# Second edge stage of a four-layer graph network: VectorE scales the gathered rows of group g + 2 ahead of the last sums of group g

## The reference, cut to what matters

```python
norm_src = clip(out_deg, 1) ** -0.5
h = nfeat * norm_src[:, None]
agg = segment_sum(h[src], dst)             # over 25000 edges
conv = agg @ W * norm_dst[:, None] + b     # norm_dst = clip(in_deg, 1) ** -0.5
sfeat = (nfeat @ W + b) / (in_deg + 1)
esum = segment_sum(efeat @ We + be, dst)
out = conv + sfeat + esum / clip(in_deg, 1)
```

## Time and profile before

| | us |
|---|---|
| median of 3 runs | 12018.62 |
| lowest, highest | 12002.51, 12023.15 |
| profiled execution | 11995.85 |
| its span on the core | 11994.1 |
| mean granted TensorE clock | 0.687 |

### The profile page before, as it was taken

How to read it: one execution, slowest core, us unless ns; L and a number is a source line. 1 busy time by engine, 2 the same in 40 slices (tenths; PEclk the granted TensorE clock), 3 DMA queues, 4 the chain that set the end, 5 groups by cost and what they waited for, 6 DMA issues and landing times. The chain is left out here.

```text
span 11994.1 us, 149789 instructions
## 1 busy us (share of the span) xinstructions
PE 6782.4 (57%) x33931; PEld 5074.2 (42%) x33931; DVE 6277.9 (52%) x20811; ACT 1432.6 (12%) x3027; POOL 6513.3 (54%) x6508
## 2 busy tenths in 40 slices
PE   3544547665567656567656667655567266570072
PEld 2333214443356444356443446544346144560051
DVE  5576545555545555545555554555554755550067
ACT  0022003000002000001100000200000500351005
POOL 4667351555643556553455654356554555676646
PEclk8755767766677766667776667776667577785555
DMA  3143001344422344421334431334431511692106
GB/s 121 38 159 122 2 2 54 70 82 83 84 47 65 69 79 84 82 56 40 87 76 83 84 63 30 92 73 84 83 72 31 181 48 52 146 200 37 24 20 267
DMA packets 526027, 950.80 MB, mean 79 GB/s; under 512 B 187011, under 2 KB 269788, under 8 KB 525604
## 3 DMA queue, kind: packets, MB, share of 16 engines
q0 software_dynamic: 192000, 330.22, 18.4%
q1 hardware_dynamic: 316196, 516.19, 13.8%
q10 hardware_dynamic: 17664, 102.61, 2.1%
HBM read 502.28 MB, written 458.64 MB: 80 GB/s over the span
## 5 line engine op out<-in xcount | busy, mean ns | idle before, releaser
L965 POOL DMA_INDIRECT G<-tab,gidx x4000 | 3805.8, 951 | 3554.8 <-issue 1897.5
L1401 PE MATMUL PS<-G,M 128*128 128x128 f32 x8000 | 2131.7, 408 | 1945.6 <-DVE G L396 1626.8
L1401 PEld LDWEIGHTS PS<-G,M 128*128 128x128 f32 x8000 | 1722.9, 276 | 2402.2 <-DVE G L396 1827.1
L1386 PE MATMUL PS<-G,lring 128*1 128x128 f32 x8000 | 1498.3, 348 | 224.9 <-DMA G<-tab,gidx 184.4
L398 DVE SCALAR_TENSOR_TENSOR G<-G,whole,PS 1x128 f32<-1x128 f32 (+1 forms) x3300 | 1103.5, 334 | 823.7 <-issue 128.2
L1346 DVE TENSOR_TENSOR Y<-PS,big 128x512 f32<-128x512 f32 x800 | 553.4, 692 | 1334.0 <-remote 1079.2
L419 DVE TENSOR_SCALAR M<-keyrow,keycol,wccol 128x128 f32 (+1 forms) x4004 | 1135.3, 364 | 29.3 <-issue 8.2
L1386 PEld LDWEIGHTS PS<-G,lring 128*1 128x1 f32 x8000 | 719.6, 100 | 779.7 <-DMA G<-tab,gidx 226.7
L1355 ACT COPY big<-PS 128x512 f32 x200 | 117.0, 585 | 5453.5 <-remote 3647.8
L1397 PE MATMUL PS<-M,G 128*128 128x128 f32 x1600 | 486.3, 401 | 437.9 <-DVE G L396 431.6
L1066 POOL DMA_INDIRECT Y<-pair_d,G x400 | 402.3, 1006 | 359.7 <-DMA pair_d<-UT 207.4
(11 more groups left out here) (498 smaller groups left out, 11639.0 us busy)
## 6 DMA issues: line engine op xcount, KB each, us to landing
tab<-Y SPq DMA_DIRECT2D x1000, 256.0 KB
big<-agg SPq DMA_DIRECT2D x90, 832.0 KB, 12.7
G<-tab,gidx POOLq DMA_INDIRECT x4000
big<-x SPq DMA_DIRECT2D x60, 832.0 KB, 8.8
xt_d<-big SPq DMA_DIRECT2D x30, 858.0 KB, 13.6
x2n<-big ACTq DMA_DIRECT2D x30, 838.5 KB
big<-x2n SPq DMA_DIRECT2D x30, 838.5 KB
agg<-big ACTq DMA_DIRECT2D x30, 832.0 KB
```

Source lines behind the costliest of these rows:

```text
L965: pool.indirect_dma_start(G[:, t % RG, 0:D], None, tab_in(k), bass.IndirectOffsetOnAxis(ap=gidx[:, t:t + 1], axis=0)).then_inc(l_got[t % R ...
L1386: nc.tensor.matmul(PS[0:1, CAR, j, :], lring[:, GR * h + j:GR * h + j + 1], G[:, s, 0:D], start=True, stop=True).then_inc(l_row, 1)
L1401: ins = nc.tensor.matmul(PS[:, SUM + h, j, :], M[:, GR * h + j, :], G[:, s, 0:D], start=True, stop=True)
```

## The change

VectorE's order in this stage is written out. `normed(0, 0)`, `summed(0, 0)` and `normed(0, 1)` stand ahead of the loop. In the loop, for each g: `summed` of g + 1, a wait for c_sum of g, `normed` of g + 2, `finished` of g. Behind the loop: `summed` of group 49, `finished` of 48 and of 49. The other engines' programs stay as they are.

```diff
-                def to_sums(i, h):
-                    normed(i, h)
-                    summed(i, h)
-                two_stages(dve, to_sums, finished)
+                normed(0, 0)
+                summed(0, 0)
+                normed(0, 1)
+                with dve.Fori(0, IT - 1) as i:
+                    for h in range(2):
+                        summed(i + h, 1 - h)
+                        steady(dve, 2 * i + h + 1)
+                        dve.wait_ge(c_sum, 2 * i + h + 1)
+                        normed(i + 1, h)
+                        finished(i, h)
+                summed(IT - 1, 1)
+                finished(IT - 1, 0)
+                finished(IT - 1, 1)
```

## The result

The kernel after took 12139.5 us (median of 4 runs, 12124.9 to 12145.4), the kernel before 12020.9 beside it: a ratio of 1.0098, with a 95% interval of 1.008 to 1.0115, so some 96 to 138 us slower. The forecast was 12151 us.

A forecast was written before the change was run, and what follows sets the result against it. No engine is full, so a loop of waits sets the pace; the change closes it in one group, 16.69 us against 13.88, 47 times: +132 us on the median scale's 12018.6, 12151 us, range 12100 to 12222.

The forecast's parts named there:

- The loop: Second edge stage: Y, scatter, gather, landing, scaling, last sums, Y close in one group, 16.69 us against 13.88; chance 0.77.
- first scatter to last gather: POOL's issues in the loop, from the first scatter to the start of the last gather: 9.05 us.
- gather to scaling: Start of the last gather on POOL to VectorE's scaling of its tile: 2.53 us.
- scaling and index copy: VectorE's scaling of the last tile plus the small copy L1694: 0.38 us.
- bound of 4.05 us for the landing: Upper end of gather start to scaling, from the stage's start; would add 71 us, giving 12222.
- The sum: Whole change: 2.81 us a group, 47 times, +132 us, with the ends' +1.0 and -1 cancelling.
- Both ends: Ahead of Y of group 0, +1.0 us for one more scaling; Y of 47 to Y of 49, -1 (0 to -2.5).
- The added wait: VectorE's wait for c_sum of g before scaling g + 2: costed at 0, if c_sum comes within 8.6 us of Y.
- late signals of TensorE: Rival: TensorE's late signals set the new pace, 20.2 us a group, +298 us, 12317 us; chance 0.11.
- room that a loop of 16.7 us leaves: VectorE's running sums have 4 us before the first gathered tile, 8 before the last; L1718 about 13 us from Y.
- The gather is already there: Rival: VectorE never stands for gathered rows; POOL's issues, 10.34 us a group, set the floor: -166 us, 11852; chance 0.05.
- From Y of g - 1 to the scaling of g + 2 there are two groups of time, one of them slack: Claim on the kernel before: its POOL-VectorE loop spans two groups, so the gather is always early (10.7 us of waits).

The follow-up runs named there:

- experiment 5: Kernel after with the scaling of g + 2 behind the last sums of g again, the added c_sum wait kept: 0.9989 of the kernel before, period 14.15 us.
- experiment 1: Kernel after with POOL gathering one group further ahead, gather of g + 3 before scatter of g: 1.0074 of the kernel before, period 15.68 us.
- experiment 4: Kernel before with only two of each group's four tiles scattered: 0.9939 of the kernel before, period 12.75 us.
- experiment 8: Kernel of experiment 1 with SP's loads of edge rows left out from group 2 on: period 14.70 us, stretch 690.9 us.

## Why the prediction was right

*The loop.* It is as worked out, term by term. Measured in the turn above: Y, which ends at 10010.84 + 1.14 = 10011.98, to scatter 0.83 (0.84 forecast); first scatter to last gather 9.01 (9.05); gather to scaling 2.55 (2.53); scaling and index copy 0.27, since L1712 starts before the copy has ended (0.38); up to L1718 0.62 (0.60); to the end of Y 3.28 (3.29). Sum 16.56, forecast 16.69, mean over 47 groups 16.64. The bound of 4.05 us for the landing was not needed.

*The sum.* 129.8 us in the stretch, 132 forecast. From the first gather to Y of group 0 it took 1.6 us more (26.2 against 24.6), 1.0 forecast; from Y of 47 to Y of 49 it took 3.0 less (14.1 against 17.1), where I had -1 with -2.5 as the end. Both ends missed, and in part cancel. Together 128 us. The medians differ by 119, and the interval of 96 to 138 holds both. The two profiled executions differ by 149, of which 21 lie before this stage's first gather, where the program is the same.

*The added wait.* Cost nothing, as forecast: experiment 5.

*Rivals.* VectorE doesn't wait for late signals of TensorE in the kernel after (1.8 and 1.4 us), as argued from the room that a loop of 16.7 us leaves; experiment 1 shows such waits as soon as the room is gone, at 15.7 us a group and not at the 20.2 that I priced from one pair of periods. "The gather is already there" was priced at POOL's own issues, 10.34 us, as if nothing else stood close behind. That was the weak step: with the gather there, TensorE's signals stop the stage at 15.7.

*What I had wrong.* "From Y of g - 1 to the scaling of g + 2 there are two groups of time, one of them slack" holds for the gather alone. I read the wait ahead of L1718 as TensorE's, noted that it came 4.9 us after the start of TensorE's record, and did not see that it came near the end of POOL's DMAs. So the old period, too, went with one group's scatters and gathers, closed by c_wm in the place of the landing, if not one for one (experiment 4). This misreading didn't touch the sum, which sets the new loop against the measured old period; that the sum came out is not owed to it. In these terms the change is 2.8 us a group slower because landing, scaling and L1712 to L1718 now follow the last gather's issue (2.55 + 0.27 + 0.62 = 3.44 us), where L1718 followed after 0.22 us in rows 4 and, by the mean period, after 13.88 - 0.84 - 9.01 - 3.33 = 0.70.

## What to carry to other kernels

Before moving a consumer ahead of a producer on one engine, write down the loop that it closes over *all* queues: here Y, scatter, gather, scaling, Y, and count how many groups long it is; a wait of 10.7 us in the old profile says nothing of the slack in a loop that is one group shorter. With POOL's order changed to suit it, and a pause, the reordered kernel has the lowest median here of those that do all the work (11944.6 us); but the old order with the same change on POOL has 11959.8 with an overlapping interval, so what gained there was POOL's order, and no run shows a gain of the reordering itself. Where a wait in the profile has no visible cause, look at what ends at the same moment on the other engines.

## What the runs showed of the hardware that was not expected

TensorE's semaphore updates can reach the waiting engines late while POOL issues indirect DMAs back to back. By its records in the kernel before, TensorE's sums are through at 9918.3 and ScalarE, which waits for them, starts at 9922.58:

```profile
9918.03 0.28 PE L1781 MATMUL PS<-big,M 128*128 x2
...
9922.58 0.58 ACT L1747 COPY big<-PS 128x512 f32<-128x512 f32 x1 [4.92 <-remote]
```

The delay was 4.3 us there (the view says "remote"; in the code ScalarE waits there for c_sum). Over the 50 groups the median from the end of TensorE's record of these sums to ScalarE's start is 3.6 us in the kernel before, 0.27 without gathers and 0.06 without scatters. VectorE's signals show no such delay: Y to the scatter took 0.83 to 0.84 us in the rows shown.

Not every signal in a series is late. In the same group VectorE has all four last-row sums (L398) 0.25 us after TensorE's record of them ends at 9910.42 + 3.33 = 9913.75, 3.0 us into POOL's series, which began at 9911.00:

```profile
9910.42 3.33 PE L1768 MATMUL PS<-big,lring 128*1 128x128 f32 x16 [5.99 <-DVE big L1692]
...
9914.00 0.47 DVE L398 SCALAR_TENSOR_TENSOR big<-big,whole,PS 1x256 f32<-1x256 f32 x1 [1.89 <-PE PS L1768]
```

Nor does it take a pause of POOL to end the delay. In the kernel before, where it issues eight DMAs in a series, ScalarE starts 2.27 to 2.59 us after the start of the last gather in 43 of 47 groups. That is about what a gather takes to land (2.53 us in rows 6). In experiment 1, 18 of the 28 starts of ScalarE that are over 1 us late fall inside a series, as the one at 10205.38 does, and in experiment 8, 20 of 30. So "the signals come when POOL pauses" is too simple, and which part of POOL's work holds them, the issuing or the transfers, no run here tells.

Whether TensorE itself runs later than its records say, or only its signals do, one stretch of the kernel before answers in part:

```profile
9982.17 0.39 PE L1791 MATMUL PS<-big 128*128 128x128 f32 x2
...
9984.85 0.28 PE L1781 MATMUL PS<-big,M 128*128 x2
...
9987.24 1.12 DVE L1718 SCALAR_TENSOR_TENSOR big<-big,PS 128x128 f32<-128x128 f32 x4 [3.64 <-DMA x2n<-big]
...
9988.18 0.58 ACT L1747 COPY big<-PS 128x512 f32<-128x512 f32 x1 [4.81 <-remote]
```

Between the end of the products (9982.56) and the end of the next group's sums (9985.13) lie 2.57 us of TensorE's work, but their waiting engines start 0.94 us apart. If the sums took as long as recorded, the signal of the products was some 1.6 us late by itself, with the work done. For the rest of the delay the question stays open.
